# A fused attention and spiking feed-forward kernel: the feed-forward's first product on pairs of tiles instead of fours, the last batch's M built later, the opening of phase two written out

## The reference

```python
x = x + attn(layernorm(x), Wq, Wk, Wv, Wo, bo)      # 16 heads of 64
x = x + ffn(layernorm(x), W_fc, W_proj)

# attn: linear attention
q = elu(x @ Wq) + 1;  k = elu(x @ Wk) + 1;  v = x @ Wv
z   = einsum('bhnd,bhd->bhn', q, k.sum(axis=2)) + 1e-6
out = einsum('bhnd,bhde->bhne', q, einsum('bhnd,bhne->bhde', k, v)) / z
return out @ Wo + bo

# ffn: y drives five steps of a leaky spiking neuron
h = square(relu(x @ W_fc.T))                        # 1024 wide
y = h @ W_proj.T
mem = 0.9 * mem + y - (mem > 1);  spike = mem_new > 1     # five times
return spikes.sum() / 5
```

## Time and profile before

| | us |
|---|---|
| median of three runs (1072.05 to 1073.37) | 1072.98 |
| profiled execution | 1073.83 |
| its span | 1072.0 |
| TensorE busy | 1033.4 |
| VectorE busy | 900.8 |
| ScalarE busy | 714.9 |
| GpSimd busy | 654.2 |
| granted clock of TensorE, mean | 0.992 |

### The profile page before, as it was taken

The page is one execution under the profiler, slowest core; times in us unless marked ns, Lnnn a source line. Parts: engine busy times, 40 slices in busy tenths (PEclk is TensorE's granted clock), DMA queues, the critical chain, the costliest instruction groups (busy, mean ns, idle before and its releaser), DMA issues.

```text
span 1072.0 us, 18793 instructions
## 1 busy us (share of the span) xinstructions
PE 1033.4 (96%) x6596; PEld 617.4 (58%) x6596; DVE 900.8 (84%) x1871; ACT 714.9 (67%) x1209; POOL 654.2 (61%) x404
## 2 busy tenths in 40 slices
PE   7999999999999997779999999999999999999997
PEld 4444444444444464556566767666676766667766
DVE  6899888897988678799888898888888888888856
ACT  6788677777778636646676766667676666767562
POOL 1443434364345436848878787787878778787732
PEclk9999999999999998999999999999999999999999
DMA  5445543224324313444454554545445454553411
GB/s 138 133 124 148 107 119 94 64 66 116 96 60 104 98 26 85 89 108 102 96 128 103 96 111 90 116 90 109 103 96 115 87 115 85 113 100 84 100 40 35
DMA packets 263086, 104.15 MB, mean 97 GB/s; under 512 B 217296, under 2 KB 260432, under 8 KB 262992
## 3 DMA queue, kind: packets, MB, share of 16 engines
q1 hardware_dynamic: 262992, 102.96, 43.4%
HBM read 33.69 MB, written 16.79 MB: 47 GB/s over the span
## 4 chain that ended last, share of the span: by engine, by line
PE 78%; DVE 10%; ACT 4%; POOL 3%; issue 3%; DMA 1%; SPq 1%; ACTq 0%; DVEq 0%; POOLq 0%
PE proj L530 25%; PE acc L675 13%; PE acc L558 13%; PE acc L653 13%; PE acc L640 12%; DVE spikes L1074 2%; DVE feat L919 1%; POOL h L1187 1%; POOL feat L1167 1%; DVE feat L994 1%; DVE zsum L998 1%; ACT feat L726 1%; DMA xT<-xnat 1%; ACT h_f L845 1%; ACT feat L730 1%
## 5 line engine op out<-in xcount | busy, mean ns | idle before, releaser
L726 ACT ACTIVATE feat<-proj 128x1024 f32<-128x1024 f32 x108 | 110.6, 1024 | 219.0 <-PE proj L530 196.4
L1187 POOL TENSOR_TENSOR h<-h_f,h 128x512 f16<-128x512 f32 x128 | 146.2, 1163 | 147.0 <-ACT h L851 147.0
L1153 POOL TENSOR_TENSOR qT<-qT,feat 128x1024 f32<-128x1024 f32 x44 | 103.7, 2357 | 142.5 <-DVE xnat L914 122.3
L675 PE MATMUL acc<-wpT,h 128*128 128x256 f16 x1536 | 180.6, 275 | 9.4 <-DVE spikes L1074 9.3
L653 PE MATMUL acc<-xn2T,wfcT 128*128 128x512 f16 x768 | 177.5, 381 | 6.9 <-DVE m_all L980 6.4
L530 PE MATMUL proj<-xn2T,xT 128*128 128x512 f16 x768 | 177.8, 382 | 4.8 <-DMA xT<-xnat 4.6
L640 PE MATMUL acc<-m_all,qT 128*128 128x256 f16 x1488 | 172.4, 273 | 4.3 <-DMA qT<-feat 4.3
L558 PE MATMUL acc<-feat,xnat 128*128 128x512 f16 x768 | 176.2, 379 | 0.0
L675 PEld LDWEIGHTS acc<-wpT,h 128*128 128x128 f16 x1536 | 150.9, 99 | 31.5 <-DVE spikes L1074 12.0
L530 PE MATMUL proj<-wq,xT 128*128 128x512 f16 x720 | 165.2, 379 | 1.0 <-DMA xT<-xT_spill 0.5
L640 PEld LDWEIGHTS acc<-m_all,qT 128*128 128x128 f16 x1488 | 145.4, 98 | 34.5 <-DMA qT<-feat 5.3
(11 more groups left out here) (93 smaller groups left out, 1273.1 us busy)
## 6 DMA issues: line engine op xcount, KB each, us to landing
x_t<-in_L_attn_x_dram SPq DMA_DIRECT2D x128, 128.0 KB, 2.3
xT_spill<-xT SPq DMA_DIRECT2D x64, 128.0 KB, 2.0
out_dram<-out_t SPq DMA_DIRECT2D x64, 128.0 KB, 2.1
xT<-xT_spill SPq DMA_DIRECT2D x60, 128.0 KB, 2.3
ks_all<-ks_rows SPq DMA_DIRECT2D x4, 512.0 KB, 4.2
m_all<-in_L_attn_Wk_dram SPq DMA_DIRECT2D x4, 256.0 KB, 4.2
xT<-xnat SPq DMA_TRANSPOSE x64, 2.4
m_all<-in_L_ffn_W_fc_dram SPq DMA_DIRECT2D x4, 256.0 KB, 3.4
```

Of the source, the lines that this page charges most:

```text
L675: mm = pe.matmul(y_at(n), h[:, c % 2, left, f, u * P:(u + 1) * P], wpT[:, right, f::FB, :], start=(i == 1), stop=(i == FB * len(PRODUCTS)))
L726: act.activation(dst, proj[:, place, :], ACT.Relu, scale=-1.0 / QK_SCALE).then_inc(neg, 1)
L1187: pool.tensor_tensor(h[:, c % 2, LO, f, :], h_f[:, k % 4, :], h[:, c % 2, HI, f, :], ALU.subtract).then_inc(h_lo, 1)
```

## The change

- *f1 on pairs.* `f1_group(k)` makes two f blocks of one pair of tiles (256 columns each) into one bank; four groups are a pair, two of them a step. Relu, square, h_hi and h_lo work on 128x512 as before. h is half as large, xn2T holds four pairs. f1 of tile n comes at step n + 7 (was n + 9), f2 at n + 9 (was n + 13). ScalarE's seed and VectorE's Newton steps are made for two tiles at once, and normalise, xn_hi, xn_lo and turn_xn2 come in twos, in every second step.
- *Memory.* h and x2 are half as large; wk, wo, kvT, a fourth feat have places of their own. G lives in two batches' space, so copy_g of batch 2 and 3 waits for the kv job of two batches before.
- *Last batch's M.* kv is a guest ahead of q 7, the two M jobs ahead of q 25 and q 28 (`LATE`), in slots of proj.
- *The first steps* (up to t = 8) are written out on every engine; the loop starts at t = 9.

```diff
-        h = sb("h", [P, 2, 2, FB, HALF], F16)
+        h = sb("h", [P, 2, 2, FB, 2 * P], F16)
-        x2 = sb("x2", [P, 16 * D], F32)
-        wo = x2[:, 8 * D:8 * D + PAIRS * D].rearrange("p (j n) -> p j n", j=PAIRS)
+        x2 = sb("x2", [P, 8 * D], F32)
+        wo = sb("wo", [P, PAIRS, D], F32)
-        xn2T = sb("xn2T", [P, 2, 2 * C2, HALF], F16)
+        xn2T = sb("xn2T", [P, 4, 2 * C2, 2 * P], F16)
-        feat = sb("feat", [P, 3, HD], F32)
+        feat = sb("feat", [P, 4, HD], F32)
...
-        USERS += [("q", n) for n in range(EARLY, TILES)]
+        LATE = {7: ("kv", B - 1, 0), 25: ("m", B - 1, 0), 28: ("m", B - 1, 1)}
+        for n in range(EARLY, TILES):
+            if n in LATE:
+                USERS.append(LATE[n])
+            USERS.append(("q", n))
...
         def f1_step(n):
-            return n + 6 if n < 4 else n + 9
+            return min(n + 7, TILES + 5)
         def f2_step(n):
-            return n + 10 if n < 4 else n + 13
+            return n + 9
-        STEPS = range(3, TILES + 16)
+        STEPS = range(FILLED, TILES + 11)          # FILLED = 9
...
+            def f1_group(k):
+                pair, g = k // 4, k % 4
+                if g == 0:
+                    for n in (2 * pair, 2 * pair + 1):
+                        pe.wait_ge(xn2T_ready[n % 4], 16 * (n // 4 + 1))
+                wait_past(pe, h_relu, k - 1)
+                for f in (2 * g, 2 * g + 1):
+                    i = 0
+                    for c2 in range(C2):
+                        for left, right in PRODUCTS:
+                            i += 1
+                            mm = pe.matmul(acc[:, 2 + g % 2, f % 2 * 2 * P:(f % 2 + 1) * 2 * P],
+                                           wfcT[:, left, f * C2 + c2, :], xn2T[:, pair % 4, right * C2 + c2, :],
+                                           start=(i == 1), stop=(i == C2 * len(PRODUCTS)))
+                mm.then_inc(f1_done, 1)
...
+            pe.wait_ge(g_copied[0], 2 * B)         # TensorE's first steps
+            o_tile(0)
+            o_tile(1)
+            o_tile(2)
+            guest_job("kv", B - 1, 0)
+            o_tile(3)
+            q_tile(7)
...
+            f1_half(0)
+            q_tile(8)
+            f1_half(1)
+            o_tile(4)
+            q_tile(9)
+            f1_half(2)
+            o_tile(5)
+            f1_half(3)
...
             def q_exp_tile(n):
                 act.wait_ge(q_proj, n + 1)
-                wait_past(act, q_lo, n - 1 if n < EARLY else n - 2)
+                wait_past(act, q_lo, n - 1 if n < EARLY else n - 3)
...
+            for t in STEPS:                        # VectorE
+                spiking = at(f2_step, t - 1)
+                for n in at(o_step, t - 2):
+                    if n % 2:
+                        lo_pair(n // 2)
+                for k in range(5):
+                    if live(t):
+                        Q_STEPS[k](t)
+                    if k == 0 and t + 1 in LATE:
+                        m_lo_job(*LATE[t + 1][1:])
+                    for n in spiking:
+                        spike_step(n, k)
+                for n in spiking:
+                    write_out(n)
+                for n in at(o_step, t - 1):
+                    if n % 2:
+                        normal_pair(n // 2)
+                for n in at(o_step, t):
+                    fresh(n)
```

More of the change, by code:

```diff
@@ new lines, in f1_half, with f2_tile @@
+            def f1_half(n):
+                for k in blocks_of(n):
+                    f1_group(k)
+            def f2_tile(n):
+                pair, u = n // 2, n % 2
+                last = n == TILES - 2
+                if u == 0:
+                    pe.wait_ge(h_lo, 4 * (pair + 1) - last)
+                if n == 0:
+                    pe.wait_ge(x2_done, 6)
+                if n == TILES - 5:
+                    pe.wait_ge(x2_done, TILES)
+                wait_past(pe, spike_steps, 5 * (n - (n > TILES - 6)))
@@ L649, in f1_block @@
                 i = 0
-                for c2 in range(C2):
+                for f in range(FB):
+                    if last and f == FB - 2:
+                        pe.wait_ge(h_lo, 4 * (pair + 1))
                     for left, right in PRODUCTS:
                         i += 1
-                        mm = pe.matmul(acc[:, 2 + f % 2, :], wfcT[:, left, f * C2 + c2, :], xn2T[:, c % 2, right * C2 + c2, :],
-                                       start=(i == 1), stop=(i == C2 * len(PRODUCTS)))
@@ L655, in f1_block @@
[L655 to L675 removed]
+                        mm = pe.matmul(y_at(n), h[:, pair % 2, left, f, u * P:(u + 1) * P], wpT[:, right, f::FB, :],
@@ new lines, in seed_pair, with h_hi_of @@
+            def seed_pair(pair):
+                u = 2 * pair % 4
+                act.wait_ge(ln2.stats, 2 * pair + 2)
+                act.activation(logv[:, u:u + 2], mv[:, u:u + 2, 1], ACT.Ln, bias=eps[:, :]).then_inc(ln2.log, 1)
+                act.wait_ge(ln2.log, pair + 1)
+                act.activation(seed[:, u:u + 2], logv[:, u:u + 2], ACT.Exp, scale=-0.5).then_inc(ln2.seed, 1)
+            def h_hi_of(n):
+                for k in blocks_of(n):
+                    square_block(k)
+                for k in blocks_of(n):
+                    h_hi_block(k)
@@ L874, in _ @@
[L874 to L881 removed]
+                    if n % 2:
+                        seed_pair(n // 2)
+                if t + 1 in LATE:
+                    m_hi_job(*LATE[t + 1][1:])
+                if live(t + 1):
+                    q_exp_tile(t + 1)
@@ new lines, in normal_pair, with lo_pair @@
+            def normal_pair(pair):
+                newton_pair(pair)
+                normalise(ln2, x2_at(2 * pair), 2 * pair)
+                normalise(ln2, x2_at(2 * pair + 1), 2 * pair + 1)
+            def lo_pair(pair):
+                xn_lo(ln2, 2 * pair)
+                xn_lo(ln2, 2 * pair + 1)
+            q_elu_tile(4)
+            sum_of_q(4)
+            q_elu_tile(5)
+            sum_of_q(5)
+            dve.wait_ge(k_added, TILES)
+            fresh(0)
+            copy_g(B - 1)
@@ new lines, in _ @@
+            fresh(1)
+            q_elu_tile(6)
+            normal_pair(0)
+            fresh(2)
+            lo_pair(0)
+            take_ks(B - 1)
+            take_kv(B - 1)
+            fresh(3)
+            sum_of_q(6)
+            normal_pair(1)
+            q_elu_tile(7)
+            lo_pair(1)
+            sum_of_q(7)
+            q_elu_tile(8)
+            sum_of_q(8)
+            fresh(4)
+            fresh(5)
+            for t in STEPS:
+                spiking = at(f2_step, t - 1)
+                for n in at(o_step, t - 2):
+                    if n % 2:
+                        lo_pair(n // 2)
@@ L1126, in _ @@
                     write_out(n)
-                if t >= 7:
-                    for n in normal:
-                        newton(ln2, n)
-                        normalise(ln2, x2_at(n), n)
-                    for n in fresh:
-                        residual(n)
-                        stats_b(n)
+                for n in at(o_step, t - 1):
+                    if n % 2:
+                        normal_pair(n // 2)
+                for n in at(o_step, t):
+                    fresh(n)
         @block.gpsimd
```

312 lines of the change are left out of this document (167 added, 145 removed).

## The result

| | before | changed |
|---|---|---|
| median, first comparison | 1072.76 (1072.05 to 1073.37, 4 runs) | 1064.87 us (1062.29 to 1065.91, 4 runs) |
| ratio | | 0.9923, 95% interval 0.9903 to 0.9943 |
| profiled execution, its span | 1073.83, 1072.0 | 1062.29, 1060.5 |
| o tile 0 starts, TensorE ends | 383.20, 1066.56 | 381.16, 1055.03 |
| phase two on TensorE, the difference | 683.36 | 673.87 |

The forecast was 1059.6 us, with 1049 to 1070 as the range. Time and direction hold; the median is 5.3 us above the forecast, so 7.9 of the forecast's 13.4 us came. Of the 11.5 us between the two spans, 9.5 came in phase two, which the change rewrites.

The account below looks back on a forecast made before the run. TensorE was taken as the bound, busy 1033.4 of 1072.0 us, with 30.4 us lost in phase two. 1036.2 without waits plus 17.0 of losses plus 5.4 for last spikes and store: span 1058.6, time 1059.6 us, range 1049 to 1070.

Parts of the forecast that it names:

- o tile 2, f1 tile 0, f1 tile 3, f2 tile 1: Opening of phase two: TensorE waits for residual 0, turned pair 0, relu of tile 2, spikes of tile 0; sum 8.1 us.
- slow clock behind the longest wait: Opening: after one long wait f2's products run partly at 1.2 instead of 2.4 GHz, 1.4 us more.
- guest at step 24: Late M job: q 25 waits for elu 24, behind a pair's low parts on VectorE; 2.1 us.
- guest at step 27: Second late M job: no pair's low parts in front, elu ends at 0.9, so no wait, 0 us.
- lumps in 26 pairs: Steady steps: two tiles' low parts and normalising fall in one step; 0.08 us for each pair, 2.0 us.
- tail: End of phase two: f1 of tile 62 stands 13 us behind o of tile 63; 0.5 us, spikes 0.
- late in each pair: Rival, steady steps: VectorE just too late, 0.6 us in each of 26 pairs, 15.6 us, time 1073; chance 0.06.
- the rival's 55 us: Rival, steady steps: a normalising slip loses VectorE's lock with GpSimd twice, 2.1 us per pair, time 1113; chance 0.05.
- nearly clean: Rival: opening has only the f2 wait, lumps cost nothing; losses 5 to 8 us, about 1049; chance 0.10.
- Moved waits: Rival: ScalarE, GpSimd, VectorE each late by one more block; opening sum 16, two slow stretches, 1069 us; chance 0.08.
- Weight loads in the open: Rival, f1 in pairs: 768 weight loads of 98 ns uncovered, 75 us, time 1133; chance 0.01.
- the lock: VectorE and GpSimd shut each other out of VectorE operations on two SBUF operands; example 2.06 instead of 1.2 us.

Follow-up runs that it names:

- the low parts apart: Changed kernel with VectorE's two xn_lo subtractions of a pair no longer back to back, the second behind q's elu and the first spike step: 1061.24 us, ratio 0.9894.
- M behind the spikes alone: Changed kernel with VectorE's part of a late M job behind the pair's spikes, the two low-half subtractions still together: 1063.17 us, ratio 0.9905.
- The longer step: Changed kernel with one more VectorE operation of 0.67 us in each pair, behind the elu: 1070.27 us, ratio 0.9982.
- the second profile: Profile of the unaltered changed kernel's repetition, run for its scatter: 1064.56 us, ratio 0.9928; phase two takes 675.2 us.
- the spikes first: Changed kernel with tile 0's five spike steps and output ahead of the pair's low parts and q tile 10 at step 10: 1064.03 us, ratio 0.9924.
- M a step later: Changed kernel with the first late M job ahead of q tile 26 instead of 25: 1065.16 us, ratio 0.9935.
- the run with halves: Kernel before with f1 in two halves of 256 columns, 24 products per block instead of 12 of 512: 1074.22 us, ratio 1.0018.
- the low parts apart and M early: Changed kernel with the two low-half subtractions apart and the M jobs at steps 10 and 11 instead of 25 and 28: 1062.1 us, ratio 0.9905.

## Why the prediction was right, by its own steps

The account from o tile 0 to the last product holds 653.0 us of work. Predicted on top of it: 17.0, measured: 673.87 - 653.0 = 20.9.

| step | predicted | measured |
|---|---|---|
| f1 in pairs | 1.9 | 1.9 (alone, on the kernel before) |
| o tile 2, f1 tile 0, f1 tile 3, f2 tile 1 | 0.2, 1.2, 2.4, 4.3 = 8.1 | 0, 1.68, 1.12, 4.37 = 7.2 |
| slow clock behind the longest wait | 1.4 | 4.25 - 2.79 = 1.5 |
| stops of the pipeline, 0.16 each | 1.0 (six) | 1.4 (nine) |
| guest at step 24 | 2.1 | 2.10 |
| guest at step 27 | 0 | 1.50 |
| lumps in 26 pairs | 2.0 | about 0.3 |
| tail | 0.5 | 0.32 + 1.84 + 0.62 + 1.18 = 4.0 |

The measured terms sum to 19.8. The remaining 1 us of the 20.9 is not waiting: between o tile 0 and the last product TensorE idles 673.87 - 659.04 = 14.8 us, and the nine waits of the table are 14.7 of it. About 0.6 is in the account itself: its step of 10.41 us is a sum of rounded rows, while the steps of the kernel before repeat every 10.42 us, 57 times. The other 0.4 is open.

*The opening and q tile 25* were walked forward from the rows of before, and the sum came out within 1 us. Part of that is luck: f1 tile 3 was put 1.3 too high and f1 tile 0 0.5 too low, and the largest wait was not worked out but taken over from the same place of before, 4.39. The runs show what it is made of: with the low parts apart 2.55 of the 4.37 us are left. The slow clock behind it came as forecast in the first profile (4.25 us of products), but took 4.46 in the second and 5.30 with M behind the spikes alone. The prediction put it down to the longest waits; in the kernel before the third longest of phase two, 3.86 us, had none, and a shorter one, 2.66, had it:

```profile
445.19 2.79 PE L640 MATMUL acc<-m_all,qT 128*128 128x256 f16 x24 [3.86 <-DMA qT<-feat]
...
529.28 4.12 PE L675 MATMUL acc<-wpT,h 128*128 128x256 f16 x24 [2.66 <-DVE spikes L1074]
```

*The steady steps* have a margin of 0.27 us, where the prediction had 0.2. The rows that it shows do not give that 0.2: from the end of the elu to the last spike they have 715.91 - 711.27 = 4.64 us, and 713.6 + 4.64 = 718.2 leaves nothing. In the changed kernel this stretch takes 717.61 - 713.19 = 4.42, since q_times_ks, which GpSimd's q_lo had held for 1.68 us, now comes later and takes 1.45. The margin held in nearly every pair (one step of 10.70 us), so the 2.0 us for the lumps were too much. The longer step shows how little "late in each pair" was away: 0.67 us more is enough to lose in every pair.

*The tail* is the mis-sized term, 4.0 for 0.5, and the second guest, 1.5 for 0, the other. The largest wait of the tail and the guest's go through one event, and the text had it only in its rival, as a case for all 26 pairs or none: a slip of VectorE that brings Newton or normalise onto GpSimd's h_lo. What makes VectorE late differs. At the guest it is M's 1.66 us and a wait of 1.49 for ScalarE's half. In the tail TensorE's step has no q any more and takes 7.86 us instead of 10.45, while VectorE still has all the work of q tile 63; f2 at 998 already waits 0.32 for its spikes. At 999 to 1004 us of the changed kernel:

```profile
999.13 1.11 DVE L1185 SCALAR_TENSOR_TENSOR newt<-mv,seed 128x2 f32<-128x2 f32 x1
1000.18 2.13 POOL L1279 TENSOR_TENSOR feat<-feat 128x1024 f16<-128x1024 f32 x1
1000.27 2.06 DVE L1188 SCALAR_TENSOR_TENSOR newt<-newt,seed 128x2 f32<-128x2 f32 x1
1002.26 1.90 POOL L1271 TENSOR_TENSOR feat<-feat,rz 128x1024 f32<-128x1024 f32 x1
1002.36 1.82 DVE L1191 SCALAR_TENSOR_TENSOR newt<-newt,seed 128x2 f32<-128x2 f32 x1
```

o at 1005 waits 1.84 us for the residual behind these, and f2 at 1008 0.62. The 1.18 at 1015 are another matter: q_lo of tile 63 stands on GpSimd behind two h_lo blocks, of which the first waits for ScalarE until 1008.07, and ends at 1012.6. Behind the guest at step 27 the two normalises took 3.34 us, beside h_lo and q_lo, and f2 waited at 634:

```profile
621.97 2.27 POOL L1300 TENSOR_TENSOR h<-h_f,h 128x512 f16<-128x512 f32 x2 [4.50 <-ACT h L885]
623.18 3.34 DVE L982 TENSOR_SCALAR xn<-x,mv,newt 128x256 f32<-128x256 f32 x2
624.20 2.18 POOL L1279 TENSOR_TENSOR feat<-feat 128x1024 f16<-128x1024 f32 x1
```

The guest's wait went in the run with M behind the spikes, and o's 1.84 in the one with Newton's steps for one tile at a time. For the other waits of the tail the account rests on the rows alone. The slip does not go on for all pairs, against the rival's 55 us: once TensorE has waited, VectorE is early again. The rival's point of decision was right and its reach was wrong.

*By halves that cancel*: 2.0 us of the changed kernel's first profile came ahead of phase two, where the forecast had none. Without it the span would be 1062.5 and the time, about 1.8 us more than the span in every run, 1064.3, near the medians of 1064.9 and 1064.6. So the forecast was 5 us low: 3.9 in the account above, and 675.2 - 653.0 - 17.0 = 5.2 by the second profile, whose phase two has 1.7 us of slow products behind q tile 25 besides.

*The rivals*: nearly clean (1049) fell by f2 tile 1. Moved waits (1069) was wrong as a time, but the attempts to remove one wait by itself showed its mechanism: the spikes first, M a step later and the low parts apart each moved a wait on. Weight loads in the open fell by the run with halves.

## What to carry over

When TensorE is full but for a few waits, list for each wait what stands ahead of the awaited operation on its engine; work that nobody needs soon (here M's 1.66 us) belongs behind the operation on which TensorE waits, and its place in the program then hardly matters. Removing one wait by itself often moves it, so try pairs of edits, for the waits that they leave each other: 3.3 and 1.4 us alone were 8.5 together, while the low parts apart and M early, 3.3 and 2.8 alone, were 2.5 together. Look for the place where two engines' queues slip against each other, at guests, at the start and at the end, and price the lock there as a single event of 2 to 4 us, even where the steady step is free of it. Where one engine's work ends and the others' goes on, as in the tail, work out the shorter step anew.
